# DeepFM with CIN on one core: the last sum of a tile by four one-column products instead of a fold and one

## The chip, the cores and the metric

The kernel runs on 1 core of one Trainium2 chip. The metric is the device time of one execution in microseconds (us). Before the change the median of 3 runs is 490.32 us (490.31 to 490.58).

## The reference

For 2048 rows of 26 indices the model gathers 26 embeddings of 16 numbers and a first-order weight each, and adds four results: the first-order sum, the factorization machine, a small network with two hidden layers of 400, and a CIN of three layers. The parts that matter here:

```
emb = embed_table[f_ix, x_idx]
lin1 = w1_table[f_ix, x_idx].sum(axis=1, keepdims=True) + w1_bias
fm = 0.5 * ((s * s).sum(-1) - (emb * emb).sum(axis=(1, 2)))[:, None]
x0 = emb.transpose(0, 2, 1)
for W in (cin_w0, cin_w1, cin_w2):
    last = jnp.einsum('ndl,ndf,klf->ndk', last, x0, W)
    feats.append(last)
cin_out = jnp.concatenate(feats, axis=-1).sum(axis=1)
cin_result = cin_out @ lin_w + lin_b
```

## The kernel before

The CIN and the factorization machine are sums over a cubic form in x (the 26 numbers of one embedding position). The kernel folds the three CIN weights once, at the start, into a matrix over pairs of fields. Then it goes through 16 tiles of 128 rows.

In a tile, the 16 positions are treated in four quarters q of 4 positions (512 columns: 4 positions by 128 rows), and the pairs of fields in three chunks c. That gives 12 steps u = 3q + c. For each step TensorE forms the sums of pairs ("pick", `picked`, line 1093, into one of three banks `ps_s`), three steps ahead. ScalarE squares them (`square`, lines 598 to 605; for c = 2 also a copy, line 600; for c = 0 also a square kept in `left`, line 604). VectorE subtracts to get the low half of the square, `z_lo` (line 803), because the products are made in a reduced float32 with a high and a low half. TensorE multiplies by the folded weights (`main`, lines 1106 to 1108, and for c = 1 the third-order part, lines 1113 to 1115).

After each quarter VectorE multiplies the result by what was kept in `left` (`times_left`, line 814) and adds it to a running sum (`add_product`, line 829). The last of these sums, `prod_sum` (127 partitions by 512 columns: four quarters of 128 rows), has to be summed over partitions and over its four quarters of 128 columns; the result is one number for each of the 128 rows. Before the change VectorE folds the four quarters into one tile of 128 columns (`fold`, lines 844 to 850), in the next tile at step 4, and TensorE, at step 6 of that next tile, multiplies the folded tile by a column of ones (`sum_products`, line 1126). Float32 products of this kind appear in the trace as two passes, each with its weight load. The last tile's sum is different: `sum_last` (line 1137) has 12 one-column products over three parts and no fold.

Beside this run the two hidden layers (`hidden1`, `hidden1_transposed`, `hidden2`), the gathers of embeddings on GpSimd (line 506; 26, 24 and then 22 per tile, 358 in all, four tiles of buffers), and the look-ups: the last four fields of most tiles aren't gathered but found by a one-hot product. For these, VectorE makes the one-hot table (line 934), TensorE multiplies (`look_rows`, lines 1192 and 1193, after steps 0, 3, 6 and 9), and VectorE picks the row (lines 945 and 949).

For the next tile ScalarE copies the gathered rows into order by position (`copy_by_position`, line 578, ahead of `square(10)`), which waits for the tile's gathers and look-ups; TensorE transposes them (`x_all`, line 1081, at step 9); ScalarE and VectorE make their high and low halves (lines 584 and 796), and ScalarE copies the whole x (lines 590 and 591) once the low halves are ready. TensorE's pick for step 2 of the next tile waits for that copy.

The order on each engine is fixed by the program text: each engine has its own list, and semaphores connect them. At the end of a tile VectorE's list is `start_tile` (lines 901 and on), for the last tile `start_last` (line 887).

Of the kernel before, what the change touches and what calls it, by code (L numbers as in the profile page):

```python
# [11 lines left out]
ALU = mybir.AluOpType  # L12
ACT = mybir.ActivationFunctionType
AX = mybir.AxisListType

P = 128
BANK = 512
QUAD = BANK // P
# [79 lines left out]
def deepfm_cin_kernel(nc, x_idx, rows, w1_bias, mlp_w1, mlp_b1, mlp_w2, mlp_b2, mlp_w3, mlp_b3,  # L98
# [7 lines left out]
    T = N // P  # L106
# [5 lines left out]
    NROW = NW + 1  # L112
# [10 lines left out]
    NQ = 4  # L123
# [11 lines left out]
    YCOL = BANK - T  # L135
# [3 lines left out]
    with ExitStack() as ctx:  # L139
        def sb(name, shape, dt=F32):  # L140
            return ctx.enter_context(nc.sbuf_tensor(name, shape, dt))

        def psum(name):
            return ctx.enter_context(nc.psum_tensor(name, [P, BANK], F32))

        def sem(name):
            return ctx.enter_context(nc.semaphore(name))
# [29 lines left out]

        room_a = sb("room_a", [P, F * F + F * (F + 1)])
        left = room_a[:, 0:2 * BANK].rearrange("p (q n) -> p q n", q=2)
        folded = room_a[:, 2 * BANK:2 * BANK + P]  # L180

        sums = sb("sums", [P, 3 * BANK])
        acc = [sums[:, q * BANK:(q + 1) * BANK] for q in range(2)]
        prod_sum = sums[:, 2 * BANK:3 * BANK]
# [94 lines left out]
        ones = sb("ones", [P, 1])  # L279
# [11 lines left out]
        ps_y = psum("ps_y")  # L291
# [36 lines left out]
        x32_ready = sem("x32_ready")  # L328
        quad_done, q_bank_free = sem("quad_done"), sem("q_bank_free")
        third_done, prod_ready, y_done = sem("third_done"), sem("prod_ready"), sem("y_done")  # L330
        tri_prod, tri_added, prod_added, folds = sem("tri_prod"), sem("tri_added"), sem("prod_added"), sem("folds")
        h1_zeroed = sem("h1_zeroed")
        h1_done, h1_ready, h1t_done = sem("h1_done"), sem("h1_ready"), sem("h1t_done")
        h1t_hi_ready, h1t_lo_ready = sem("h1t_hi_ready"), sem("h1t_lo_ready")
# [26 lines left out]
        def look_at(t, slot):  # L361

            n = LOOKS * t + slot
            if n < AHEAD:
                return (FIRST_LOOK - 1, n)
            m = n - AHEAD
            return (FIRST_LOOK + m // LOOKS, m % LOOKS) if n < look_no(T, 0) else None
# [341 lines left out]
        def _(dve):  # L709
# [83 lines left out]
            def x_low(t, h):  # L793
                dve.wait_ge(hi_ready, x_no(t, h) + 1)
                rs, to = slice(LO * h, LO * (h + 1)), slice(LO * (1 - h), LO * (2 - h))
                dve.tensor_tensor(xt[t % 2][to, h], x_bank(t)[rs, :].rearrange("p (c n) -> p c n", c=4),
                                  xt[t % 2][rs, h].bitcast(F32), ALU.subtract).then_inc(lo_ready, 1)

            def z_low(t, u):
                k = CK[u % NC]  # L800
                dve.wait_ge(hi_ready, s_no(t, u) + 1)
                ps = s_bank(t, u)[0:k, :]
                z = dve.tensor_tensor(z_lo[0:k, u % NC, :], ps, z_hi[0:k, u % NC, :].bitcast(F32), ALU.subtract)  # L803
                if t == T - 1 and u == 0:

                    dve.wait_ge(prod_ready, NQ * t - 1)
                    dve.tensor_scalar(left[0:k, 0, :], ps, 1.0, None, ALU.mult).then_inc(lo_ready, 1)
                else:
                    z.then_inc(lo_ready, 1)

            def times_left(t, q):
                dve.wait_ge(quad_done, NQ * t + q + 1)
                ps = ps_q[q % 2][0:NROW, :]
                dve.tensor_tensor(ps if q else acc[0][0:NROW, :], ps, left[0:NROW, q % 2, :],  # L814
                                  ALU.mult).then_inc(prod_ready, 1)
                if q == 0:
                    dve.nop().then_inc(q_bank_free, 1)

            def sum_of(q):
                return acc[q % 2] if q < NQ - 1 else prod_sum  # L820

            def add_product(t, q):
                dve.wait_ge(prod_ready, NQ * t + q + 1)
                if q == 3:
                    dve.wait_ge(tri_added, t + 1)
                    dve.wait_ge(q_bank_free, NQ * t + q)
                    if t:
                        dve.wait_ge(folds, t)
                dve.tensor_tensor(sum_of(q)[0:NROW, :], ps_q[q % 2][0:NROW, :], acc[(q - 1) % 2][0:NROW, :],  # L829
                                  ALU.add).then_inc(q_bank_free, 1)  # L830

# [6 lines left out]
            def add_third(t):  # L838
                s = acc[(NQ - 2) % 2][0:NROW, :]
                dve.wait_ge(tri_prod, t + 1)  # L840
                dve.wait_ge(q_bank_free, NQ * t + NQ - 1)
                dve.tensor_tensor(s, ps_t[0:NROW, :], s, ALU.add).then_inc(tri_added, 1)

            def fold(t):

                dve.wait_ge(q_bank_free, NQ * t + NQ)
                if t:
                    dve.wait_ge(y_done, t)
                dve.tensor_reduce(folded[0:NROW, :], prod_sum[0:NROW, :].rearrange("p (j n) -> p n j", j=QUAD), AX.X,
                                  ALU.add).then_inc(folds, 1)  # L850

            def hidden1_low(t):
                dve.wait_ge(h1t_hi_ready, t + 1)
                dve.tensor_tensor(h1t_rest[0:HR], ps_mlp[0:HR, 3 * P:BANK], h1t_rest[0:HR].bitcast(F32),
                                  ALU.subtract)
                dve.tensor_tensor(h1t_lo[:], ps_mlp[:, 0:3 * P].rearrange("p (c n) -> p c n", c=3),
                                  h1t_hi[:].bitcast(F32), ALU.subtract).then_inc(h1t_lo_ready, 1)
# [6 lines left out]
            def tile(t):  # L864
                for u in range(NC, NU):
                    q = u // NC - 1
                    if u % NC == 2:
                        times_left(t, q)
                    z_low(t, u)
                    if u == NU - 1 and t + 1 < T - 1:  # L870
                        x_low(t + 1, 0)
                    if u % NC == 2 and q:
                        add_product(t, q)
                    if u == 4 and 0 < t < T - 1:
                        fold(t - 1)
                    if u == 7:
                        hidden1_low(t)
                    slots = PICKED if t else PICKED_0
                    if u in slots and look_at(t, slots[u]):
                        pick_row(*look_at(t, slots[u]))  # L880
                    if t == 0 and u - 1 in LOOK_SPLIT:
                        look_low(LOOK_SPLIT[u - 1])
                    slots = KEYS if t else KEYS_0
                    if u in slots and look_at(t, slots[u]):
                        keys_to_one_hot(*look_at(t, slots[u]))

            def start_last():
                t = T - 1
                times_third(t - 1)
                times_left(t - 1, NQ - 1)  # L890
                x_low(t, 0)
                x_low(t, 1)
                hidden2(t - 1)
                z_low(t, 0)
                add_third(t - 1)
                z_low(t, 1)
                add_product(t - 1, NQ - 1)
                z_low(t, 2)
                fold(t - 1)

            def start_tile(t):
                if look_at(t - 1, LOOKS - 1):
# [94 lines left out]
                    start_last()  # L997

            dve.wait_ge(third_done, T)
            dve.wait_ge(folds, T - 1)  # L1000
            dve.wait_ge(q_bank_free, NQ * T - 1)
            dve.tensor_tensor(acc[1][0:NROW, :], ps_t[0:NROW, :], x32[(T - 1) % 2][0:NROW].rearrange("p c n -> p (c n)"),
                              ALU.mult).then_inc(tri_added, 1)
# [14 lines left out]
        def _(pe):  # L1018
# [3 lines left out]
            for g in range(F):  # L1022
                mm = pe.matmul(ps_y[:, g:g + 1], w2[:, :, g], lin[:, 2:3], start=True, stop=True)
# [5 lines left out]
            for f in range(F):  # L1029
                c = (f % HALF) * (F + 1)  # L1030
                mm = pe.matmul(ps_q[f // HALF][:, c:c + F + 1], w1[:, :, f], m_lin2[:], start=True, stop=True)
# [12 lines left out]
            def swapped(mat, c, n, m):  # L1044
# [11 lines left out]
                      start=True, stop=True).then_inc(y_blocks, 1)  # L1056
            pe.matmul(ps_s[2][0:F, 0:NX_], bp[:, LINO:NCOL], ap_[:, X1:XE], start=True, stop=True)
            for c, n, m in ((X1, N1, N2), (X2, N1, N3), (X3, N2, N3)):
                o = NX_ + c - XO
                mm = pe.matmul(ps_s[2][0:F, o:o + n * m].rearrange("p (b a) -> p b a", a=n), bp[:, LINO:NCOL],  # L1060
                               swapped(ap_, c, n, m), start=True, stop=True)
            mm.then_inc(yl_block, 1)
            for g, ps in enumerate((ps_q[0], ps_q[1], ps_t)):
                ws = slice(WO[g], WO[g] + ORD[g])
                pe.matmul(ps[0:ORD[g], 0:NCOL], ap_[:, ws], bp[:], start=True, stop=False)
                mm = pe.matmul(ps[0:ORD[g], XO:LINO], bp[:, ws], ap_[:, XO:LINO], start=False, stop=True)
# [54 lines left out]
            def sum_products(t):  # L1121

                if looked_by(t + 1):
                    pe.wait_ge(looked, looked_by(t + 1))
                pe.wait_ge(folds, t + 1)
                pe.matmul(ps_y[:, YCOL + t:YCOL + t + 1], folded[0:NROW, :], ones[0:NROW, :],
                          start=True, stop=True).then_inc(y_done, 1)

            def sum_last():
                t = T - 1  # L1130
# [73 lines left out]
            for n, col, k in blocks:  # L1204
                if n != 3:
                    o, j = by_row_ps(n)[0:k, ROW1:NROW], n if n < 3 else n - 1
# [4 lines left out]
            for g in range(3):  # L1211
                pe.wait_ge(total_ready, g + 1)
                for n, col, k in (blocks[0], blocks[3], blocks[2], blocks[1], blocks[5], blocks[4]):
                    mm = pe.matmul(by_row_ps(n)[0:k, 0:NW], total[0:ORD[g], g, col:col + k], to_sq[0:ORD[g], g, 0:NW],
                                   start=False, stop=(g == 2 and n in (1, 4)))
# [11 lines left out]
            for g in range(3):  # L1227
# [3 lines left out]
                      stop=True).then_inc(za_done, 1)  # L1231
# [63 lines left out]
```

## Time and profile before

| | us |
|---|---|
| median of 3 runs | 490.32 |
| profiled execution, its own time | 490.69 |
| its span, first to last instruction | 488.9 |
| TensorE busy | 454.1 |
| VectorE busy | 414.0 |
| ScalarE busy | 369.8 |
| GpSimd busy | 343.3 |
| 15 folds on VectorE | 16.0 |

The span is the time between the first and the last instruction; the execution's own time has some 1.8 us around it. The busy times overlap: engines work side by side, so none of these adds to another. A matmul's duration in the rows is longer than the distance to the next one, since matmuls are pipelined; the distance of their starts tells what one costs. "idle before <-" names what ended an engine's idle time.

### The profile page before, as it was taken

To read this page: it belongs to the slowest core of one execution; us is meant where nothing else is said; L and a number is where in the kernel's file an instruction comes from. 1 tells how busy PE (TensorE), PEld (TensorE's weight loads), DVE (VectorE), ACT (ScalarE), POOL (GpSimd) and SP (SyncE) were. 2 spreads that over 40 slices of the span, in tenths; PEclk is the share of its full clock that TensorE was granted. 3 is DMA by queue.
4 is the path that set the end of the run, shared out by engine and by line. 5 is a ranking of instruction groups with operands and counts; after the bars stand their busy time and mean duration, and the time that the engine had idled before them with its cause. 6 is when DMAs were issued, how large, how long until landed. Compare 5 with 4: busy or idle time off the path is not lost.

```text
span 488.9 us, 6838 instructions
## 1 busy us (share of the span) xinstructions
PE 454.1 (93%) x2179; PEld 383.0 (78%) x2179; DVE 414.0 (85%) x873; ACT 369.8 (76%) x726; POOL 343.3 (70%) x363
## 2 busy tenths in 40 slices
PE   0998987889999999999999999999999999999998
PEld 0995665678888888888888888888888887878666
DVE  6163369799999999999999989999999999999876
ACT  0063496588988888888888888888888878888894
POOL 5777778777777777777777777777777777777200
PEclk9999999899999999999999999999999999999999
DMA  8963694222222222222222222222222222222100
GB/s 169 215 158 28 93 223 149 8 7 8 8 8 8 7 9 7 9 8 8 8 8 7 8 8 8 7 8 8 8 8 9 7 9 7 8 7 10 3 0 2
DMA packets 21602, 15.64 MB, mean 32 GB/s; under 512 B 12786, under 2 KB 19903, under 8 KB 21439
## 3 DMA queue, kind: packets, MB, share of 16 engines
q0 software_dynamic: 11456, 3.14, 18.8%
q1 hardware_dynamic: 7106, 10.05, 8.2%
q10 hardware_dynamic: 3005, 2.01, 2.1%
q8 instruction: 18, 0.29, 0.2%
q14 instruction: 17, 0.14, 0.1%
HBM read 14.97 MB, written 0.21 MB: 31 GB/s over the span
## 4 chain that ended last, share of the span: by engine, by line
POOL 66%; issue 21%; PE 5%; ACT 5%; DVE 1%; DMA 1%; POOLq 0%; DVEq 0%
POOL emb L506 66%; ACT ps_s L605 1%; ACT z_hi L598 1%; PE ps_q L1106 1%; ACT z_hi L600 1%; PE ps_q L1108 1%; PE ps_q L1107 1%; PE ps_y L1137 1%; DMA emb<-rows,idx_raw 0%; DMA idx_raw<-x_idx 0%; PE ps_s L1093 0%; DVE z_lo L803 0%; PE ps_y L1192 0%; PE ps_y L1193 0%; ACT room_a L604 0%
## 5 line engine op out<-in xcount | busy, mean ns | idle before, releaser
L506 POOL DMA_INDIRECT emb<-rows,idx_raw x358 | 343.0, 958 | 111.7 <-issue 108.8
L803 DVE TENSOR_TENSOR z_lo<-ps_s,z_hi 128x512 fp32r<-128x512 f32 (+1 forms) x192 | 131.1, 683 | 30.7 <-ACT ps_s L605 29.8
L598 ACT ACTIVATE z_hi<-ps_s 128x512 fp32r<-128x512 f32 (+1 forms) x192 | 113.9, 593 | 34.1 <-PE ps_s L1093 33.7
L605 ACT ACTIVATE ps_s<-ps_s 128x512 f32<-128x512 f32 (+1 forms) x192 | 113.3, 590 | 0.8
L1106 PE MATMUL ps_q<-z_lo,zw_hi 128*127 128x512 f32 (+1 forms) x192 | 79.5, 414 | 7.4 <-DVE z_lo L803 4.1
L1192 PE MATMUL ps_y<-look_hi,one_hot 128*128 128x442 f32 x232 | 85.0, 366 | 0.8 <-issue 0.8
L1093 PE MATMUL ps_s<-xt,pick 128*128 128x512 f32 (+1 forms) x192 | 76.9, 403 | 5.9 <-ACT x_two L591 5.2
L1193 PE MATMUL ps_y<-look_lo,one_hot 128*128 128x442 f32 x232 | 82.1, 355 | 0.0
L1107 PE MATMUL ps_q<-z_hi,zw_lo 128*127 128x512 f32 (+1 forms) x192 | 75.6, 394 | 0.0
L1108 PE MATMUL ps_q<-z_hi,zw_hi 128*127 128x512 f32 (+1 forms) x192 | 75.6, 394 | 0.0
L1106 PEld LDWEIGHTS ps_q<-z_lo,zw_hi 128*127 128x127 f32 (+1 forms) x192 | 36.0, 188 | 21.3 <-issue 11.5
L604 ACT ACTIVATE room_a<-ps_s 128x512 f32<-128x512 f32 x63 | 37.6, 597 | 17.4 <-DVE sums L814 12.3
L1093 PEld LDWEIGHTS ps_s<-xt,pick 128*128 128x128 f32 (+1 forms) x192 | 35.6, 186 | 19.0 <-DVE z_lo L803 10.1
L1192 PEld LDWEIGHTS ps_y<-look_hi,one_hot 128*128 128x128 f32 x232 | 44.3, 191 | 5.6 <-issue 1.6
L1193 PEld LDWEIGHTS ps_y<-look_lo,one_hot 128*128 128x128 f32 x232 | 44.2, 191 | 3.8
L934 DVE TENSOR_SCALAR one_hot<-w_space,tables 128x128 fp32r<-128x128 f16 x208 | 46.0, 293 | 0.0
L1108 PEld LDWEIGHTS ps_q<-z_hi,zw_hi 128*127 128x127 f32 (+1 forms) x192 | 35.9, 187 | 8.7
L945 DVE SCALAR_TENSOR_TENSOR ps_y<-tables,look_place,ps_y 128x442 f32<-128x442 f32 x58 | 38.9, 671 | 1.9 <-PE ps_y L1193 1.9
L600 ACT ACTIVATE z_hi<-ps_s 26x512 fp32r<-26x512 f32 x64 | 37.8, 591 | 0.7
L1107 PEld LDWEIGHTS ps_q<-z_hi,zw_lo 128*127 128x127 f32 (+1 forms) x192 | 36.1, 188 | 2.7
L949 DVE TENSOR_REDUCE emb<-ps_y 128x17 f32<-128x442 f32 x58 | 35.9, 619 | 2.0
L829 DVE TENSOR_TENSOR sums<-ps_q,sums 127x512 f32<-127x512 f32 x47 | 32.1, 682 | 0.4
(187 smaller groups left out, 684.4 us busy)
## 6 DMA issues: line engine op xcount, KB each, us to landing
emb<-rows,idx_raw POOLq DMA_INDIRECT x358, 3.0
w_space<-rows SPq DMA_DIRECT2D x2, 728.9 KB
m_space<-rows SPq DMA_DIRECT2D x2, 728.9 KB
w_space<-key_scratch SPq DMA_DIRECT2D x1, 1408.0 KB, 7.6
w<-cin_w SPq DMA_DIRECT2D x2, 416.0 KB, 4.8
w<-cin_w ACTq DMA_DIRECT2D x2, 416.0 KB, 7.5
w_space<-cin_w SPq DMA_DIRECT2D x2, 416.0 KB, 8.5
w_space<-cin_w ACTq DMA_DIRECT2D x2, 416.0 KB, 7.5
```

What stands on the lines that cost most here:

```text
L506: pool.indirect_dma_start(emb[t % EMB][:, f, :], None, rows, bass.IndirectOffsetOnAxis(row_ix[:, t, f:f + 1], 0)).then_inc(gathered[t] if ...
L598: act.activation(z_hi[0:k, c, :], ps[0:k, :], ACT.Square)
L600: act.activation(z_hi[LIN:LIN + F, c, :], ps[LIN:LIN + F, :], ACT.Copy)
L605: act.activation(ps[0:k, :], ps[0:k, :], ACT.Square).then_inc(hi_ready, 1)
L803: z = dve.tensor_tensor(z_lo[0:k, u % NC, :], ps, z_hi[0:k, u % NC, :].bitcast(F32), ALU.subtract)
L934: hot = dve.tensor_scalar(one_hot[n % 2][:, j, :], keys[:, 0, :], share_row[:, j:j + 1], None, ALU.is_equal)
L1093: pe.matmul(s_bank(t, u)[0:CK[c], :], pick[:, e, c * P:c * P + CK[c]], xt[t % 2][:, h], start=True, stop=True).then_inc(filled, 1)
L1106: pe.matmul(ps, hi_w, lo_x, start=(c == 0), stop=False)
L1107: pe.matmul(ps, lo_w, hi_x, start=False, stop=False)
L1108: mm = pe.matmul(ps, hi_w, hi_x, start=False, stop=(c == NC - 1))
L1192: pe.matmul(o, one_hot[n % 2][:, j, :], look_hi[i][:, ws], start=(j == 0), stop=False)
L1193: mm = pe.matmul(o, one_hot[n % 2][:, j, :], look_lo[i][:, ws], start=False, stop=(j == SHARES - 1))
```

## The change

VectorE's fold is gone, with its tile and its semaphore `folds`. TensorE's sum reads `prod_sum` directly: four one-column products, one for each quarter, add up in the same column of PSUM. It waits for the last addition of the tile (`q_bank_free`) where it waited for the fold; VectorE's last addition of a tile, which overwrites `prod_sum`, waits for the sum of the tile before (`y_done`) where it waited for the fold.

```diff
@@ add_product
                     if t:
-                        dve.wait_ge(folds, t)
+                        dve.wait_ge(y_done, t)
@@ fold
-            def fold(t):
-
-                dve.wait_ge(q_bank_free, NQ * t + NQ)
-                if t:
-                    dve.wait_ge(y_done, t)
-                dve.tensor_reduce(folded[0:NROW, :], prod_sum[0:NROW, :].rearrange("p (j n) -> p n j", j=QUAD), AX.X,
-                                  ALU.add).then_inc(folds, 1)
@@ tile (VectorE)
-                    if u == 4 and 0 < t < T - 1:
-                        fold(t - 1)
@@ start_last
                 z_low(t, 2)
-                fold(t - 1)
@@ end of VectorE's list
-            dve.wait_ge(folds, T - 1)
+            dve.wait_ge(y_done, T - 1)
@@ sum_products
-                pe.wait_ge(folds, t + 1)
-                pe.matmul(ps_y[:, YCOL + t:YCOL + t + 1], folded[0:NROW, :], ones[0:NROW, :],
-                          start=True, stop=True).then_inc(y_done, 1)
+                pe.wait_ge(q_bank_free, NQ * (t + 1))
+                for j in range(QUAD):
+                    mm = pe.matmul(ps_y[:, YCOL + t:YCOL + t + 1], prod_sum[0:NROW, j * P:(j + 1) * P], ones[0:NROW, :],
+                                   start=(j == 0), stop=(j == QUAD - 1))
+                mm.then_inc(y_done, 1)
```

## Rows read from the trace of the kernel before

**Rows 1.** Table by stretches: stretch, us, busy (count) of PE, PEld, DVE, ACT, POOL.
```profile
235.00:261.00 26.00, 25.66 (x125) 21.91 (x125) 24.47 (x53) 21.85 (x44) 19.60 (x22) 1.00 0.23 8
```

**Rows 2.** Timeline of VectorE in a middle tile: start, duration, operation [idle before].
```profile
238.15 1.06 DVE L849 TENSOR_REDUCE room_a<-sums 127x128 f32<-127x512 f32 x1
...
240.97 0.69 DVE L803 TENSOR_TENSOR z_lo<-ps_s,z_hi 128x512 fp32r<-128x512 f32 x1 [0.56 <-ACT ps_s L605]
...
250.46 0.68 DVE L803 TENSOR_TENSOR z_lo<-ps_s,z_hi 122x512 fp32r<-122x512 f32 x1
...
253.86 0.69 DVE L796 TENSOR_TENSOR xt<-ps_s,xt 64x512 fp32r<-64x512 f32 x1
```

**Rows 3.** Timeline of ScalarE in the same tile.
```profile
239.85 0.60 ACT L604 ACTIVATE room_a<-ps_s 128x512 f32<-128x512 f32 x1 [0.87 <-DVE sums L814]
...
241.53 0.60 ACT L598 ACTIVATE z_hi<-ps_s 128x512 fp32r<-128x512 f32 x1 [0.59 <-PE ps_s L1093]
...
247.42 0.59 ACT L598 ACTIVATE z_hi<-ps_s 128x512 fp32r<-128x512 f32 x1
...
249.62 0.57 ACT L605 ACTIVATE ps_s<-ps_s 96x512 f32<-96x512 f32 x1
...
254.58 0.60 ACT L590 ACTIVATE x<-ps_s 128x512 f32<-128x512 f32 x1
```

**Rows 4.** Timeline of TensorE in the same tile.
```profile
241.10 0.39 PE L1093 MATMUL ps_s<-xt,pick 128*128 128x512 f32 x1
...
243.63 0.28 PE L1126 MATMUL ps_y<-ones,room_a 127*128 127x1 f32 x2
243.83 0.44 PE L1192 MATMUL ps_y<-look_hi,one_hot 128*128 128x442 f32 x1
...
246.83 0.40 PE L1093 MATMUL ps_s<-xt,pick 128*128 128x512 f32 x1
247.06 0.39 PE L1106 MATMUL ps_q<-z_lo,zw_hi 122*127 122x512 f32 x1
...
255.18 0.39 PE L1093 MATMUL ps_s<-xt,pick 128*128 128x512 f32 x1
255.81 0.46 PE L1093 MATMUL ps_s<-xt,pick 128*122 128x512 f32 x1 [0.24 <-ACT x_two L591]
```

**Rows 5.** The chain of waits near 427 us: start, duration, what.
```profile
427.20 2.20 DMA emb<-rows,idx_raw
```

**Rows 6.** Timeline of ScalarE: position copies of tiles 7, 12 and 14, and what follows.
```profile
246.59 0.94 ACT L578 ACTIVATE by_pos<-emb 128x416 f32<-128x416 f32 x1
...
376.96 0.95 ACT L578 ACTIVATE by_pos<-emb 128x416 f32<-128x416 f32 x1
...
430.34 0.95 ACT L578 ACTIVATE by_pos<-emb 128x416 f32<-128x416 f32 x1 [0.94 <-issue]
431.20 0.58 ACT L598 ACTIVATE z_hi<-ps_s 128x512 fp32r<-128x512 f32 x1
```

**Rows 7.** Timeline of TensorE in the last tile.
```profile
476.21 0.28 PE L1126 MATMUL ps_y<-ones,room_a 127*128 127x1 f32 x2
476.36 0.48 PE L1106 MATMUL ps_q<-z_lo,zw_hi 128*127 128x512 f32 x1
...
477.82 0.40 PE L1093 MATMUL ps_s<-xt,pick 128*128 128x512 f32 x1
478.33 0.50 PE L1106 MATMUL ps_q<-z_lo,zw_hi 122*127 122x512 f32 x1
478.67 0.39 PE L1107 MATMUL ps_q<-z_hi,zw_lo 122*127 122x512 f32 x1
...
483.99 2.73 PE L1137 MATMUL ps_y<-ones,sums 127*128 127x1 f32 x24
```

**Rows 8.** Timeline of TensorE in tile 14, the pick for square 10.
```profile
454.83 0.40 PE L1093 MATMUL ps_s<-xt,pick 128*128 128x512 f32 x1
```

**Rows 9.** Timeline of ScalarE in tile 14, square 10.
```profile
455.94 0.60 ACT L598 ACTIVATE z_hi<-ps_s 128x512 fp32r<-128x512 f32 x1
```

More of the change, by code:

```diff
@@ L179, in deepfm_cin_kernel @@
         left = room_a[:, 0:2 * BANK].rearrange("p (q n) -> p q n", q=2)
-        folded = room_a[:, 2 * BANK:2 * BANK + P]
         sums = sb("sums", [P, 3 * BANK])
@@ L330, in deepfm_cin_kernel @@
         third_done, prod_ready, y_done = sem("third_done"), sem("prod_ready"), sem("y_done")
-        tri_prod, tri_added, prod_added, folds = sem("tri_prod"), sem("tri_added"), sem("prod_added"), sem("folds")
+        tri_prod, tri_added, prod_added = sem("tri_prod"), sem("tri_added"), sem("prod_added")
         h1_zeroed = sem("h1_zeroed")
```

## The prediction

> **What bounds the kernel now.** I read the table by stretches first, then the timelines of the three engines over one tile in the middle, and last the chain of waits around the end of tile 13.
>
> In the 26 us of one middle tile TensorE is busy 25.66 us, VectorE 24.47 and ScalarE 21.85, at a granted clock of 1.00 [rows 1]. Neither of the first two has much room, so the question is which of them carries the loop at which point.
>
> The position copies of tiles 7 and 12 start at 246.59 and 376.96: 130.37 us for five tiles, 26.07 us each [rows 6]. Where does that period come from? The reader can follow a loop through the rows. VectorE's fold starts at 238.15 and the product behind it is what ScalarE waits for, 0.87 us, before its extra square at 239.85 [rows 2, 3]. But at 241.53 ScalarE waits again, 0.59 us, for TensorE's pick of 241.10 [rows 3, 4]: whatever the fold takes from ScalarE here is waited for a second time anyway. From 240.97 on, where VectorE had its last idle time in this tile, it works without a pause up to the low half of x, 253.86 to 254.55 [rows 2]; ScalarE's full copy of x starts at once, at 254.58 [rows 3], and TensorE stands after its pick of 255.18 until 255.81 waiting for it [rows 4]. From 255.81 TensorE runs back to back to the same place of the next tile. So the loop now is: TensorE from 255.81 to the pick that is 241.10 in this tile, ScalarE and VectorE from there to 254.55, ScalarE, TensorE. The fold is in it only by VectorE's backlog in the second part.
>
> Beside the loop runs GpSimd, which issues its gathers without ever waiting. At the end of the kernel it is late: the chain of waits passes from a gather (427.20, landed 429.40) to the copy of tile 14 [rows 5], which starts at 430.34 after 0.94 us of idle [rows 6]. Without the gathers that copy would have come at 376.96 + 2 x 26.07 = 429.10. The square behind it, 0.86 us later, stands at 431.20 instead of 429.96: 1.24 us belong to the gathers, and any earlier gain in the loop ends there.
>
> **Part 1, fold removed (VectorE).** 15 folds of about 1.0 us each (1.06 by [rows 2]) go. First half of a tile: ScalarE's 0.87 us wait at 239.85 goes, and its wait at 241.53 grows by as much. Nothing gained; TensorE covers it. Second half: VectorE stands 1 us earlier and catches up with ScalarE, whose results its operations need. The last low half of z (250.46 now) can't start before ScalarE's last square is done: 249.62 + 0.57, and 0.04 for the signal (254.55 to 254.58 here), 250.23 [rows 2, 3]. That is the whole gain of the fold in the loop: 0.23 us a tile, not 1.06, and only if ScalarE is on time.
>
> **Part 2, three more products (TensorE).** A float32 product of one column is two passes in the trace. The 24 passes of the last sum take 2.73 us: 0.11 us a pass [rows 7]. Six more passes are 0.66 us. Part of it falls into a wait: between the sum and the first look-up product lie 0.20 us (243.63 to 243.83) [rows 4], against 0.15 where nothing else is awaited (476.21 to 476.36) [rows 7]; the rest is a wait that TensorE has there anyway. So x = 0.61 us here. Bounds for the six: from below 0.45, since the two passes at 476.21 are followed by the next product after 0.15, 0.075 each; from above 0.84, since the same two passes have a duration of 0.28 together, 0.14 each [rows 7]. I take 0.11, the row with the most passes of just this operation; the ends stand for x from 0.40 to 0.79.
>
> The Trainium skill, in "TensorE: Matmul & The Clock Gate", section "Back-to-back issue gap", gives for one to 64 columns about 60 cycles, some 25 ns, between products. The same page, section "LDWEIGHTS (loading the stationary operand)", gives columns / 1.2, 107 ns for 128. The row agrees with the second; by the first the six passes would cost 0.15 us, x would be 0.09, and the kernel would stay where it is.
>
> Who is behind the sum on TensorE? The look-up products, main product 7 and then the pick for square 10, at 246.83 [rows 4]. ScalarE needs it at 247.42 [rows 3]. From the start of a pick to a waiting ScalarE are 0.43 us (241.10 to 241.53), so it is ready at 247.26: slack 0.16. With x it is ready at 247.87, and the square starts 0.45 late. ScalarE has no pause from there to 249.62 + 0.57 = 250.19. So the last low half of z starts at 250.19 + 0.45 + 0.04 = 250.68 against 250.46: **the tile gets 0.22 us longer**. In one formula: x - 0.39. The gain of part 1 is in it. TensorE itself would have started its pick of 255.81 at 255.18 + 0.23 (the distance from 246.83 to its successor), 0.40 us earlier [rows 4]; even if it loses all of x on the way it comes only 0.21 late, so it asks for no more than this. In other tiles the gap before the look-up products is a little larger than here, so I take 0.20.
>
> **Part 3, the waits.** The sum now waits for the last addition of the tile before, which VectorE does in the start of this tile, ahead of its step 3, and TensorE comes to the sum at step 6; if it were late, TensorE's look-up products and all behind them would queue. VectorE's last addition waits for the sum of the tile before, which was issued at product 6, again long before. Both at nothing; if that cover were gone, it would be one addition, 0.7 us.
>
> **The sum.** The effect is in tiles 1 to 12 whole, 12 x 0.20 = 2.4, and in tile 13 up to the square, 0.45: 429.96 + 2.85 = 432.81 against 431.20, so 1.61 us later; the gathers are no longer awaited. Tile 14 has no look-ups at product 6: the pick for square 10 is issued at 454.83, ready 455.26, needed 455.94 [rows 8, 9]; slack 0.68 against 0.66, nothing is added, and ScalarE runs through. Tile 15 is carried by ScalarE until TensorE's product 8 at 478.33, which is now waiting for VectorE. With 0.66 more, the pick before it starts at 478.48 and the product at 478.71. Its successor came 0.34 after the start (load not hidden) and now comes 0.23 after: 478.94 against 478.67, 0.27 us, and from there TensorE is without a pause to the end [rows 7]. VectorE's fold of this tile is behind no one. Sum: 1.61 + 0.27 = **+1.9 us**. The profiled execution took 490.69 (span 488.9 and 1.8 around it) and would take 492.6; the median of the runs is 0.37 lower, so 492.2.
>
> **The rivals.**
> *The gathers still set the end.* If x is at its low end, or anywhere under 0.45 us (weight loads partly hidden), a tile grows by less than 0.06, and 429.96 + 12 x 0.06 + 0.45 doesn't pass 431.20. Then the copy of tile 14 starts at 430.34 as before, and all that is left is tile 15's 0 to 0.27: 490.3 to 490.6, not slower. This holds for every saving too: a much faster loop gives the same time. For it: the end of the kernel shows the wait. Against: x would have to be a quarter below the 0.61. 0.25.
> *TensorE is the bound altogether.* If its stall before 255.81 does not shrink when it gets later, each tile grows by all of x: 12 x 0.61 + 0.61 - 1.24 is 6.7, and with 0.66 in each of tiles 14 and 15 it is 8.0: 498.3. For it: 25.66 busy of 26.00 [rows 1]. Against: that stall waits for ScalarE [rows 4], which the missing fold lets come earlier. 0.12.
> *Faster.* Only gathers that come earlier could lift the floor, at most by the 1.24 us: 489.1, and only with x under 0.45. For it: VectorE works 1 us a tile less beside GpSimd. Against: GpSimd issues its gathers by its own list, 22 in the 26 us of the middle tile [rows 1], and no row ties their pace to the fold. 0.05.
>
> **How the numbers follow.** Forecast 0.58, the others as given; 0.03 of the forecast's lies within the bound of no change. Between no change and slower lie 0.98 us (0.2%, what can be told from no change here). The range takes the gathers' case in at its low end and x = 0.79 at the high end, where a tile grows by 0.40: 429.96 + 4.8 + 0.63 - 431.20 = 4.2, tile 14 adds 0.16 and tile 15 0.45, 495.1. So 490.2 to 495.0. Slower 0.67, same 0.28, faster 0.05.
>
> **What would show it.** In the profile after: no operation of 1.06 us on VectorE; 8 passes at the sum, 0.81 us between its start and the look-up products; ScalarE's square 10 waiting some 0.3 to 0.5 us for TensorE's pick in tiles 1 to 13, where it now waits for nothing; copies 26.3 us apart; no wait for gathers at tiles 13 and 14; TensorE's stall before its pick at 255.81 still there. It is wrong if the copies stay 26.07 or less apart, or if ScalarE doesn't wait at square 10.

## The result and the profile after

The changed kernel is slower: 494.0 us median of 5 runs (492.98 to 494.93) against 490.58 us for the kernel before in the same pairs (490.31 to 492.2), ratio 1.0053 with a 95% interval of 1.0037 to 1.007. The forecast was 492.2, with a range of 490.2 to 495.0. Two later measurements of the same kernel gave 493.49 against 491.33 (ratio 1.0052, 1.0039 to 1.0064) and 493.56 against 491.06 (1.0046, 1.0021 to 1.0071). So the change costs 2.2 to 3.4 us by the medians, 2.3 to 2.6 us by the ratios. The profiled execution took 494.0, its span is 491.4.

The busy times of the page after:

```profile
PE 459.4 (93%) x2269; PEld 394.7 (80%) x2269; DVE 403.8 (82%) x858; ACT 368.6 (75%) x726; POOL 341.6 (70%) x363
```

15 operations fewer on VectorE (873 before), 90 passes more on TensorE (2179 before). In a tile of 26.30 us (table by stretches, same columns as [rows 1]) TensorE is now busy 26.03, VectorE 23.95:

```profile
236.50:262.80 26.30, 26.03 (x132) 22.67 (x131) 23.95 (x52) 21.82 (x44) 19.90 (x22) 1.00 0.22 8
```

The same tile as in [rows 4], on TensorE (timeline). The sum has 8 passes and the look-up products start 0.81 us behind its start, where it was 0.20. The pick for square 10 is issued at 248.84:

```profile
242.49 0.39 PE L1081 MATMUL ps_s<-xt,pick 128*128 128x512 f32 x1
...
245.03 0.95 PE L1115 MATMUL ps_y<-ones,sums 127*128 127x1 f32 x8
245.84 0.45 PE L1182 MATMUL ps_y<-look_hi,one_hot 128*128 128x442 f32 x1
...
248.84 0.40 PE L1081 MATMUL ps_s<-xt,pick 128*128 128x512 f32 x1
...
257.46 0.46 PE L1081 MATMUL ps_s<-xt,pick 128*122 128x512 f32 x1 [0.27 <-ACT x_two L590]
```

ScalarE in the same tile answers to [rows 3]. Its wait for TensorE at 242.92 has grown from 0.59 to 1.57 us, since the wait for VectorE ahead of it is gone. Square 10, which waited for nothing, waits 0.58 us for the pick:

```profile
242.92 0.60 ACT L597 ACTIVATE z_hi<-ps_s 128x512 fp32r<-128x512 f32 x1 [1.57 <-PE ps_s L1081]
...
247.75 0.95 ACT L577 ACTIVATE by_pos<-emb 128x416 f32<-128x416 f32 x1
249.28 0.60 ACT L597 ACTIVATE z_hi<-ps_s 128x512 fp32r<-128x512 f32 x1 [0.58 <-PE ps_s L1081]
```

The chain of waits in this stretch (start, duration, what) shows the whole loop from that pick to TensorE's stall. There is no gap in it over 0.04 us but the last:

```profile
249.00 0.25 PE ps_s L1081
249.26 0.02 issue
249.28 0.60 ACT z_hi L597
249.88 0.49 ACT ps_s L604
...
251.49 0.58 ACT ps_s L604
252.07 0.02 issue
252.10 0.68 DVE z_lo L802
...
255.50 0.70 DVE xt L795
256.20 0.02 issue
256.23 0.60 ACT x L589
256.82 0.50 ACT x_two L590
257.32 0.14 issue
257.46 0.46 PE ps_s L1081
```

The position copies of tiles 7 and 12 start at 247.75 and 379.30: 131.55 us, 26.31 a tile, where [rows 6] give 26.07. (The middle one of the distances in tiles 3 to 11 is 26.30 in this profile and 26.28 in the next one of the same kernel.) And the copy of tile 14 comes without idle time:

```profile
379.30 0.96 ACT L577 ACTIVATE by_pos<-emb 128x416 f32<-128x416 f32 x1
...
431.86 0.95 ACT L577 ACTIVATE by_pos<-emb 128x416 f32<-128x416 f32 x1
433.37 0.60 ACT L597 ACTIVATE z_hi<-ps_s 128x512 fp32r<-128x512 f32 x1 [0.56 <-PE ps_s L1081]
```

Its last gather was issued at 425.33, 6.5 us before; in [rows 5, 6] it was 3.1.

Where did the 3.31 us between the two profiled executions go (494.0 against 490.69)? The first product of the first hidden layer marks each tile. For tiles 1, 14 and 15, before:

```profile
104.60 0.53 PE L1151 MATMUL ps_mlp<-m_hi,xt 128*128 128x400 f32 x2
...
444.66 0.52 PE L1151 MATMUL ps_mlp<-m_hi,xt 128*128 128x400 f32 x2
...
463.63 0.45 PE L1151 MATMUL ps_mlp<-m_hi,xt 128*128 128x400 f32 x1 [0.44 <-DVE by_row L861]
```

and after:

```profile
105.06 0.53 PE L1141 MATMUL ps_mlp<-m_hi,xt 128*128 128x400 f32 x2
...
446.85 0.34 PE L1141 MATMUL ps_mlp<-m_hi,xt 128*128 128x400 f32 x1
...
465.84 0.45 PE L1141 MATMUL ps_mlp<-m_hi,xt 128*128 128x400 f32 x1 [0.45 <-DVE by_row L852]
```

0.46 us ahead of tile 1, 1.73 in tiles 1 to 13, 0.02 in tile 14, 0.3 from there to the end of the span, and the rest, 0.8, outside the span (494.0 - 491.4 against 490.69 - 488.9). Of these only the second and the fourth are terms of the mechanism that was forecast.

### The profile page after: what moved, and what is told of

The parts are those of the page before. It is cut to its first block, busy times and chain, and to the rows that moved or that the text cites. A ratio compares the mean times of both kernels' runs of the same rounds, so it can differ in the third digit from the quotient of the medians.

```text
span 491.4 us, 6989 instructions
## 1 busy us (share of the span) xinstructions
PE 459.4 (93%) x2269; PEld 394.7 (80%) x2269; DVE 403.8 (82%) x858; ACT 368.6 (75%) x726; POOL 341.6 (70%) x363
## 4 chain that ended last, share of the span: by engine, by line
PE 63%; ACT 16%; DVE 13%; DMA 5%; issue 1%; SPq 0%; ACTq 0%; DVEq 0%
PE ps_y L1182 7%; PE ps_s L1081 7%; PE ps_y L1183 7%; PE ps_q L1094 6%; PE ps_q L1095 6%; PE ps_q L1096 6%; ACT z_hi L597 4%; ACT ps_s L604 4%; PE ps_mlp L1141 4%; DVE xt L795 4%; DMA w_space<-cin_w 3%; DVE z_lo L802 2%; PE ps_q L1019 2%; PE ps_y L1115 2%; PE ps_t L1103 2%; PE ps_t L1101 2%
## 5 line engine op out<-in xcount | busy, mean ns | idle before, releaser
L922 DVE TENSOR_SCALAR one_hot<-w_space,tables 128x128 fp32r<-128x128 f16 x208 | 47.4, 309 | 0.0
```

The lines of the kernel that those rows point to most:

```text
L922: hot = dve.tensor_scalar(one_hot[n % 2][:, j, :], keys[:, 0, :], share_row[:, j:j + 1], None, ALU.is_equal)
```

## The experiments

Eleven measurements were made in three groups, each beside the kernel before, which had a median of 491.33, 491.04 and 491.06 us in them. "Period" is the middle one of the distances of position copies in tiles 3 to 11 of the profiled execution.

### The changed kernel again

> The changed kernel once more, beside the kernel before on the same chip. My theory (the pick for square 10 comes late, 0.22 us a tile, less 1.24 us that the gathers had cost anyway) gives 1.9 to 2.1 us more than before, copies 26.28 us apart. The first measurement gave 3.4 more at the median; if its rest of 1.3 us (0.4 in the start ahead of the first tile, 0.8 outside the span) belongs to the change, it comes again: 3.4. If it was scatter of single executions, this comes out near 2.

493.49 us, ratio 1.0052 (1.0039 to 1.0064), period 26.28. The medians are 2.2 us apart; the ratio stands for 2.6, with an interval of 1.9 to 3.1. So the 3.4 of the first measurement was partly scatter, and the 1.9 that was forecast lies at the low end of the interval.

### The fold gone, one product

```diff
-                for j in range(QUAD):
-                    mm = pe.matmul(..., prod_sum[0:NROW, j * P:(j + 1) * P], ...)
+                mm = pe.matmul(..., prod_sum[0:NROW, 0:P], ones[0:NROW, :], start=True, stop=True)
```

> VectorE's fold is gone, and TensorE multiplies only the first quarter of the sum (the three other quarters are left out), so TensorE's work is that of before. Tests part 1 alone. My theory: copies of tiles 2 to 12 about 25.85 us apart instead of 26.07, since ScalarE's last square then holds the loop, and square 10 doesn't wait; then the gathers hold the copy of tile 14 as before (start at 430 to 431 us, idle before it 3 us and more), total within 0.5 us of before. Rival (VectorE is the bound and its fold was worth its whole 1 us): copies 25.1 us apart, the same end by the gathers. Second rival (gains and losses simply add, products 0.61 and fold -0.39): 25.68.

Period 25.64, total 489.26 us, ratio 0.9963 (0.9952 to 0.9974): faster than before. The period is neither mine (25.85) nor 25.1; the fold is worth 0.43 us a tile. And the gathers do hold tiles 12 to 14, here ScalarE's copies of 13 and 14 (timeline), 27.5 us apart. The wait isn't 3 us at tile 14 but some 1.8 us ahead of each of the last three copies. Square 10 (244.97) waits for nothing:

```profile
244.11 0.95 ACT L577 ACTIVATE by_pos<-emb 128x416 f32<-128x416 f32 x1
244.97 0.60 ACT L597 ACTIVATE z_hi<-ps_s 128x512 fp32r<-128x512 f32 x1
...
402.31 0.95 ACT L577 ACTIVATE by_pos<-emb 128x416 f32<-128x416 f32 x1 [1.80 <-issue]
...
429.80 0.95 ACT L577 ACTIVATE by_pos<-emb 128x416 f32<-128x416 f32 x1 [1.82 <-issue]
```

22 gathers at 1.25 us are 27.5: from tile 12 on this kernel runs at GpSimd's pace. My expectation that the total would be that of before was wrong, though the trace shows the floor that I had named.

### The fold kept, four products

```diff
-                pe.matmul(ps_y[...], folded[0:NROW, :], ones[0:NROW, :], start=True, stop=True).then_inc(y_done, 1)
+                for j in range(QUAD):
+                    mm = pe.matmul(ps_y[...], folded[0:NROW, :], ones[0:NROW, :], start=(j == 0), stop=(j == QUAD - 1))
+                mm.then_inc(y_done, 1)
```

> The fold stays on VectorE, and TensorE makes four one-column products of the folded tile instead of one (the sum of a tile is counted four times). Tests part 2 alone. My theory: once the three products are there, the pick for square 10 sets the tile, and it doesn't matter whether the fold is there; copies 26.28 us apart and a total as of the changed kernel, within 0.5 us. Rival (simply additive): copies 26.68 apart, some 7 us over before.

Period 26.28, total 493.85 us, ratio 1.0063 (1.005 to 1.0076). The same as the changed kernel within their scatter: with the three products in that place the fold is free, and removing it brings nothing. Square 10 waits here too:

```profile
248.03 0.94 ACT L578 ACTIVATE by_pos<-emb 128x416 f32<-128x416 f32 x1
249.25 0.60 ACT L598 ACTIVATE z_hi<-ps_s 128x512 fp32r<-128x512 f32 x1 [0.28 <-PE ps_s L1093]
```

The wait is shorter than 0.58 only because ScalarE still loses time to the fold earlier in the tile; the square starts at the same distance from the pick.

### The sum moved behind product 9

```diff
-                    if u == 6 and t:
+                    if u == (9 if after is not None else 5) and t:
                         sum_products(t - 1)
```

(The wait for finished look-ups goes up by one, as the sum stands one look-up later.)

> The changed kernel with the four products moved from behind product 6 to behind the transposes at product 9 (in the last tile to behind product 5), where both picks that ScalarE needs next are already issued and TensorE had idle time ahead of its pick for step 2 of the next tile. Same work on every engine. My theory (the place, not the amount, costs): square 10 no longer waits for a pick, copies 25.9 to 26.0 us apart, then the gathers hold the copy of tile 14 again: total as before, 490.3 to 490.8. Rival (TensorE's 0.61 us more work is the price wherever it stands): copies 26.28 or more apart, total as changed.

493.47 us, ratio 1.0046 (1.0032 to 1.0059), period 26.29: the rival's numbers, and my theory seemed to fall. But the profile shows the wait in a new place. Square 10 is on time; it is the square for step 0 of the next tile that now waits 1.99 us for its pick (1.18 in the changed kernel), and ScalarE's copy of x stands in line behind it (timeline of ScalarE):

```profile
250.87 0.58 ACT L597 ACTIVATE z_hi<-ps_s 128x512 fp32r<-128x512 f32 x1
...
256.86 0.60 ACT L597 ACTIVATE z_hi<-ps_s 128x512 fp32r<-128x512 f32 x1 [1.99 <-PE ps_s L1081]
...
258.35 0.60 ACT L589 ACTIVATE x<-ps_s 128x512 f32<-128x512 f32 x1
```

In the changed kernel the same copy (256.23) waited 0.17 us for VectorE after that square; now it has no such idle time, since the square is what is late. One late pick was exchanged for another. From this alone one couldn't tell whether place or amount matters, so the next run moves the sum behind both.

### The sum directly ahead of TensorE's own stall

```diff
@@ end of a tile, TensorE
                     picked(after, 1)
+                    if t:
+                        sum_products(t - 1)
                     picked(after, 2)
```

(In the same way ahead of the last tile; in the last tile itself behind product 5.)

> The changed kernel with the four products moved to directly ahead of TensorE's pick for step 2 of the next tile, where it stands idle for the copy of x (in the last tile behind product 5). In the run with the sum behind product 9, a different pick, for square 0 of the next tile, came late, so the sum was still ahead of something ScalarE needed. My theory (the sum costs nothing only where no pick for ScalarE is behind it before TensorE's own stall): copies about 25.8 us apart until the gathers hold them 27.5 apart, total as with the fold gone and one product, 489.3, 1.5 to 2 us under before. Rival (TensorE is full, 0.61 us more work is paid anywhere): copies 26.28 apart, total as changed, 493.5.

Period 25.90, total 489.34 us against 491.04, ratio 0.997 (0.9949 to 0.9991). Same work on every engine as in the changed kernel, 0.38 us a tile less. So the place matters: the same four products cost less here. But the amount is not free. My theory said 25.8, and the kernel with the fold gone and one product has 25.64, 0.26 less. TensorE's sum fills the time in which it had been idle and is longer than that time: the pick for step 2 starts 0.81 us after the sum, as its list allows, and no longer waits for the copy of x. In a whole tile (table by stretches) TensorE is busy 25.90 of 25.90 us: here, other than in the changed kernel, it is TensorE that is full. Timeline of TensorE, the stretch, then ScalarE:

```profile
254.81 0.39 PE L1081 MATMUL ps_s<-xt,pick 128*128 128x512 f32 x1
255.04 0.95 PE L1114 MATMUL ps_y<-ones,sums 127*128 127x1 f32 x8
255.85 0.48 PE L1081 MATMUL ps_s<-xt,pick 128*122 128x512 f32 x1
```

```profile
237.00:262.90 25.90, 25.90 (x132) 22.63 (x131) 23.78 (x53) 21.77 (x44) 19.50 (x22) 1.00 0.22 8
```

```profile
246.55 0.95 ACT L577 ACTIVATE by_pos<-emb 128x416 f32<-128x416 f32 x1
247.39 0.59 ACT L597 ACTIVATE z_hi<-ps_s 128x512 fp32r<-128x512 f32 x1
...
428.65 0.95 ACT L577 ACTIVATE by_pos<-emb 128x416 f32<-128x416 f32 x1 [0.63 <-issue]
```

Square 10 waits for nothing, and at tile 14 the gathers are awaited again, 0.63 us.

### Two products

```diff
-                for j in range(QUAD):
+                for j in range(2):
...
-                                   start=(j == 0), stop=(j == QUAD - 1))
+                                   start=(j == 0), stop=(j == 1))
```

> The changed kernel with two of the four products, in their place behind product 6 (two quarters of the sum are left out). Tests the slope. With one product copies are 25.64 us apart, with four 26.28. My theory: every pass is paid in full from the first on (0.11 us, two for each product), so 25.86. Rival (ScalarE's own chain holds the loop until the pick is later than its slack): 25.64 to 25.75, and the rest of the slope lies between two and four products.

Period 25.84, total 489.09 us, ratio 0.9955 (0.9937 to 0.9973). One, two and four products give 25.64, 25.84 and 26.28: 0.20 and 0.22 us a product, two passes of 0.11. So the slope is mine, from the first added product on. Square 10 shows the same: it starts 0.86, 1.07 and 1.53 us after the start of the copy ahead of it (tile 7), with one, two and four products. And the kernel with one product shows why there is no slack: its pick (timeline of TensorE) starts at 244.54, and 0.43 us later, at 244.97, ScalarE has just come to square 10.

```profile
244.54 0.40 PE L1081 MATMUL ps_s<-xt,pick 128*128 128x512 f32 x1
```

### The copy of tile 14 behind square 10

```diff
-                    if u == NU - 2 and t + 1 < T - 1:
+                    if u == NU - 2 and t + 1 < T - 2:
                         copy_by_position(t + 1)
                     square(t, u)
+                    if u == NU - 2 and t + 1 == T - 2:
+                        copy_by_position(t + 1)
```

> The kernel before with one thing moved: the position copy of tile 14 stands behind square 10 of tile 13 on ScalarE instead of ahead of it, so ScalarE squares while the last gather of that tile lands. Tests that the gathers held the end of the kernel before. My theory: the 0.94 us wait goes, total 0.9 to 1.2 us less than before. Rival (the wait was hidden by other work behind it): same as before within 0.3 us.

490.5 us against 491.04, ratio 0.9981 (0.9964 to 0.9998): a gain of 0.5 by the medians and 0.9 by the ratio, whose interval nearly reaches zero. In its profiled execution tile 1 began at 106.8 us, 2.2 later than in the profile of before, and there was no wait for gathers to fill. Inconclusive for the size: the interval holds both theories. The profile is a first sign that the gathers hold the kernel before only in some executions.

With the sum ahead of the stall, the same edit:

> Both: the four products directly ahead of the pick for step 2, and the copy of tile 14 behind square 10. My theory: the loop is faster (25.8 us) and one square of the wait for the gathers is filled: 1 us less than with the sum moved alone, some 488.3, about 2.5 to 3 us under before and 5 under the changed kernel. Rival (gathers of the last tile hold the end next): no more than 0.3 us under the sum moved alone.

489.24 us against 489.34 for the sum moved alone: the rival's 0.3 at most. The wait to be filled was only 0.63 us, and in the two profiles the copy itself starts at 429.00 behind the square instead of at 428.65 ahead of it. From the first product of the first hidden layer in tile 1 to that in tile 14 the two take 337.41 and 337.42 us: what the square wins is lost again behind the copy. At 0.9956 (0.9937 to 0.9974) against before it is no better than the simpler version within the intervals.

### Two gathers less

The credit of 1.24 us was the term most in doubt.

```diff
-                for f in [*range(F - LOOKS), *range(F - LOOKS + looks(t), F)]:
+                for f in [*range(2 if t == 5 else 0, F - LOOKS), *range(F - LOOKS + looks(t), F)]:
```

(and the wait for the gathers of tile 5 is lowered by two)

> The kernel before, without two of the 22 gathers of tile 5 (these two fields keep what an earlier tile left there), so that every later gather comes 2.5 us earlier and none can hold the copy of tile 14. Tests the credit of 1.24 us that the sum gave the gathers. In nine profiled executions the 310 gathers up to tile 14's last took 389.3 to 391.3 us, and the profile of before has the longest of them, so my theory now: in most executions of the kernel before the gathers hold nothing or little, and this gains 0 to 0.6 us. Rival (the credit is always there): 1.2 us less than before.

490.93 us against 491.06 for the kernel before, ratio 0.9991 (0.9964 to 1.0018): no difference that can be told. The medians are on my side, but the interval reaches 1.8 us less and so doesn't exclude the rival's 1.2. Its last copies come at the loop's pace without a wait:

```profile
405.30 0.94 ACT L578 ACTIVATE by_pos<-emb 128x416 f32<-128x416 f32 x1
...
431.37 0.94 ACT L578 ACTIVATE by_pos<-emb 128x416 f32<-128x416 f32 x1
```

In this execution they would have come so with all gathers too: the last gather of tile 14 started at 424.90, with two more before it it would have been some 2.5 us later, 427.4, and 3.1 us after that, at 430.5, is still ahead of 431.37 (an estimate from the rows of this profile and the 3.1 of [rows 5, 6]).

> The changed kernel without the same two gathers. In its profile the copy of tile 14 starts 6.5 us after the start of its last gather, where 3.1 are enough, so the gathers hold nothing: same as the changed kernel within 0.3 us, copies 26.28 us apart, and against the kernel before without the two gathers 13 times 0.21 and the last tile's 0.27, 3.0 us more. Rival: the changed kernel still waits for gathers in some executions, and this comes 0.5 us or more under it.

493.55 us, ratio 1.0044 against before (1.0019 to 1.0069), and 493.56 for the changed kernel beside it. Nothing shows that the changed kernel waits for these gathers. Without them, the two kernels lie 2.62 us apart by the medians. In the profiles, tile 1 to tile 14 takes 445.91 - 106.88 = 339.03 and 447.22 - 105.51 = 341.71 us, 2.68 apart, 0.206 a tile; with the gathers the same difference was 1.73, 0.95 less:

```profile
106.88 1.44 PE L1151 MATMUL ps_mlp<-m_hi,xt 128*128 128x400 f32 x7
445.91 1.62 PE L1151 MATMUL ps_mlp<-m_hi,xt 128*128 128x400 f32 x8
```

```profile
105.51 1.62 PE L1141 MATMUL ps_mlp<-m_hi,xt 128*128 128x400 f32 x8
...
447.22 1.08 PE L1141 MATMUL ps_mlp<-m_hi,xt 128*128 128x400 f32 x5
```

The third measurement of the changed kernel:

> The changed kernel once more, beside the two others on the same chip. My theory: 2.2 to 3.0 us over before, since the start ahead of the first tile scatters by 2.6 us from one execution to the next (tile 1 began at 104.6 to 107.2 us in nine profiles) and the gathers' credit is at most 0.6 in the middle. Rival: 1.9 as forecast, the first 3.4 being scatter.

493.56 us against 491.06, 2.5 us apart, as my theory has it; but the interval of the ratio (1.0021 to 1.0071) is 1.0 to 3.5 us and holds the rival's 1.9 as well.

## Why the prediction was right, and where a term was off

- **The loop and its place** (what bounds the kernel): right. The chain after shows the loop in the same order, pick, square 10, last low half of z, low half of x, copy of x, TensorE's stall. The moved sums show that the place decides how much is paid: with four products a tile takes 26.28 or more when a pick that ScalarE needs stands behind the sum, and 25.90 when none does before TensorE's stall, where TensorE itself is then full.
- **Part 1, the fold**: mis-sized. I gave it 0.23 us a tile, since ScalarE's last square would hold the loop at its old time. It is 0.43 (26.07 to 25.64). The part that I had priced is there: from square 10 to the last low half of z it takes 3.04 us before (247.42 to 250.46) and 2.82 with the fold gone and one product (244.97 to 247.79). But I had left ScalarE where it was between 241.53 and 247.42, and in that stretch it also waited some 0.2 us for VectorE's product of the next quarter ahead of its extra square (the difference of 0.70 between two starts in that place before, 245.57 - 244.87, to 0.50 after, 246.76 - 246.26). With the fold gone, that goes too. It did no harm to the forecast, as the pick sets square 10: the kernel with the fold and four products has the same 26.28.
- **Part 2, the products**: right. 0.11 us a pass; 0.81 from the sum to the look-ups as forecast; 0.20 to 0.22 a product by the slope. Square 10 waits 0.58, not 0.3 to 0.5, because ScalarE arrives 0.2 earlier. A tile is 0.22 longer by the working, 0.20 taken, 0.21 measured. The load time of 107 ns for 128 columns in the Trainium skill ("TensorE: Matmul & The Clock Gate", section "LDWEIGHTS (loading the stationary operand)") agrees with the distance of the passes, 2.73 us for 24; the weight loads have rows of their own, of 0.19 us each (24 loads of line 1137 before), which overlap. The 25 ns of the Trainium skill's section "Back-to-back issue gap" on the same page would have left no cost; that section gives it for an isolated product and says that in a stream with weight loads both set the distance, which the prediction left out.
- **Part 3, the waits**: right; no wait of VectorE for the sum or of TensorE for the last addition shows in the profile.
- **Tiles 14 and 15**: right. 0.02 and 0.3 measured, 0 and 0.27 forecast, and by the way forecast: in tile 15 the product behind the sum comes 0.81 us after its start instead of 0.15 (478.43 to 479.24), product 8 (480.95) follows its pick after 0.24 instead of 0.51, and its successor follows it after 0.24 instead of 0.34.
- **The gathers' credit**: the weakest term, and probably why the total is above the forecast. For the profiled execution the mechanism was right: against the run without two gathers, square 10 of tile 13 stands 1.27 us later, counted from the start of tile 1 (326.60 against 325.33), of which 1.03 are left at the start of tile 14 (340.06 against 339.03). But the profile of before is the one with the slowest gathers of all: 391.32 us from the first tile's last gather to tile 14's, against 389.3 to 390.6 in ten others. GpSimd issues its first gather at 3.8 to 3.9 us in every profile, while tile 1 starts at 104.6 us in this profile and up to 107.2 in others. An estimate from the eleven profiles with all gathers, from the start of tile 1 and the loop of before (324.5 us to tile 14's copy) and from tile 14's last gather (3.1 to 3.4 us to a waiting copy): the gathers would be awaited by 1.24 us in this one, by 0.7 in two, by 0.2 at most in a fourth, and not at all in seven. The totals fit, but don't prove it: without two gathers the kernel before gains 0.13 us, with an interval that still holds 1.24. By this the median gets 13 x 0.206 + 0.3 = 3.0 us, less a small rest of the credit; the medians gave 2.2 to 3.4, the ratios 2.3 to 2.6. I had moved a credit from one execution to the median of others.
- **The rivals**: that the gathers set the end is true in the profile of before and in those of the kernels whose loop is faster than 26.0 (fold gone and one or two products, sum moved), and in no profile of the changed kernel. "Not slower" was thus bound to x, as stated, and x was 0.6. That TensorE is the bound altogether is refuted for the changed kernel: its stall is still there (0.27 us at 257.46) and a tile grows by 0.21, not 0.61. It becomes true with the sum ahead of the stall, at 25.90 us a tile. "Faster" didn't occur for this change, but the statement that a faster loop can't make the kernel faster was wrong for the median: with the sum moved it is 1.7 us faster (ratio 0.997). The same scatter, which leaves the gathers out of most executions of before, would explain it; no run isolates that.

What stays open: the 0.8 us outside the span and the 0.46 ahead of tile 1 in the first pair of profiles. Repetition suggests scatter (the other two differences are 2.2 and 2.5), no run isolates them. Without the two gathers, where no credit is left, the profiles give 2.68 + 0.3 = 3.0 us and the medians 2.62; the 0.4 between them has no cause shown. And the lower ends of the three intervals, 1.8, 1.9 and 1.0 us, don't clearly part the 1.9 that was forecast from 3.0: that the credit is missing in the median rests on the profiles more than on the totals.

## What to carry to other kernels

When two engines are both near full, ask of moved work which operation stands behind it in the receiving engine's list and who waits for that; the same change cost 0.2 us a tile with the four products ahead of a pick that ScalarE needs, and became a gain (ratio 0.997) with them behind the last such pick before the engine's own stall. The stall is worth only its own length: once it was filled, TensorE was busy all the time and the rest of the products was paid. Moving work once to a place with idle time can only exchange one late operation for another; look through to the next stall. And a slack or a floor between two engines that start independently (here gathers against the loop) should be taken over several executions, not from one profile: here it was 1.24 us in one and, by an estimate, nothing in seven of eleven.

## What was not expected of the hardware

The time at which tile 1 begins scatters from 104.6 to 107.2 us between the profiled executions, with identical code for nearly all that precedes it (tile 0's first product of the first hidden layer already scatters from 66.8 to 70.2), and the pace of 310 gathers by 2 us (389.3 to 391.3). Together they are as large as the whole effect, while the period of the changed kernel repeats to 0.02 us (26.28 to 26.30 in four profiles, one of them without two gathers).
